# A bidirectional Mamba layer with its FFN: the last skip term moved into the state sum, one tail norm moved to VectorE, the head's first turn and projection in halves

## The chip, the cores and the metric

One NeuronCore of a Trainium2 chip. The metric is the device time of one execution in microseconds, the median of three runs. Engines are named as in the profile: PE is TensorE, PEld its weight loads, DVE VectorE, ACT ScalarE, POOL GpSimd, SP SyncE. TensorE's granted clock has two levels, 1.2 and 2.4 GHz; the profile gives it as a share of 2.4.

## The reference, cut to what matters

```python
def mamba(x, ...):                       # once forwards, once on the reversed sequence
    u, z = split(x @ in_w.T)             # 256 channels each
    u = silu(causal_conv4(u) + conv_b)
    dt, B, C = split(u @ xproj_w.T)      # rank 8, 16 states, 16 states
    dt = softplus(dt @ dt_w.T + dt_b)
    h[t] = exp(dt[t] * A) * h[t-1] + dt[t] * B[t] * u[t]     # 16 states per channel
    y[t] = sum_n(h[t, n] * C[t, n]) + D * u[t]               # D * u is the skip term
    return (y * silu(z)) @ out_w.T

xn = norm(layernorm(x)) * gamma + beta                        # x: 4 sequences x 512 tokens x 128
x = x + layernorm(layernorm(x) + mamba_f(xn) + reverse(mamba_b(reverse(xn))))
x = x + layernorm(ffn(layernorm(x)))     # ffn: (silu(x Wg) * (x Wu)) Wd, hidden 384, int weights / 127
```

All arithmetic is fp32, but for B's rows, which TensorE broadcasts as three bf16 parts.

## The kernel before, in words

**Tiling.** The work falls into 8 units, one for each sequence q and direction d (unit k = 2q + d), and each unit into 16 steps, one for each state n: 128 steps. In a step the channels lie on the partitions (two halves of 128) and the 512 positions in the free dimension, so that one VectorE scan of 128x1024 computes h for one state (L1313). Its inputs are the decay exp(dt A) from ScalarE (`exp`, L937, a ring of six) and dt B u, made in one of three ways: TensorE broadcasts row B into PSUM (`bcast`, L678, or L682 for the first four steps) and VectorE multiplies it by dt u (`mul_b`, L1294); or ScalarE scales the transposed dt u (`g`, L1048) and TensorE turns it back (`g_turn`, L705); or GpSimd multiplies (L1172). GpSimd multiplies h by C (`mul_c`, L1151), and TensorE adds the product to the sum over states by a transpose into the PSUM tile `ysum` (`fold`, L735), three steps behind the scan.

**Order.** `plan()` (L122) writes one list of stages; every engine walks through the same list and issues the stages that are its own, so the order in the list is the order in each engine's queue. `start` is the head, ahead of scan 0. `put(slot, ...)` weaves a stage in behind the scan of that step. `plan_banks()` (L306) gives each short-lived PSUM result one of the two `scr` banks, or, once the scans are over, one of six.

**Head.** The first sequence is loaded; VectorE takes the statistics, GpSimd the power -1/2, VectorE the four norms of 128 tokens each (L1377). TensorE transposes the four blocks (`turn`, L789), ScalarE scales them by gamma and beta into `xn_fwd` (L982). One half of the convolution is a plain projection (`u_raw`, L797), for which VectorE then makes the four tap passes (`conv_passes`, L1386 and L1393), the other half is four matmuls with folded taps (L809). Three warm-up matmuls (L664) stand between turn and projection, 14 ahead of the turn. ScalarE makes u (L991), TensorE the x projection (L830), ScalarE copies it to `xdbl` (L1005). Then `bc`: four small transposes of B and C (L840) and ScalarE's copy to `bc_t` (L1013); `dt_mm` (L849) and `dt` (L1021) for each half; `dtu` on VectorE (L1415). SyncE stores `xdbl` and reads C's rows back as broadcast tiles as soon as `xdbl` is read. Beside this VectorE takes the statistics of the other three sequences (`ln_var_rest`, L1369 and L1371), and GpSimd takes their powers (`ln_pow_next` L1183, `ln_pow_rest` L1187) and folds the taps of the backward direction (`fold_taps`, L1215). Behind scan 0 come `dtu_turn` (L713, L1036) and the turn of the first backward half, again L789.

**Tail.** The last two steps are scanned in two parts of 256 positions (L1332), part 1 of the tokens (blocks 2 and 3) first; `ysum` of the last unit has one bank for each part. The last c products of step 127 are VectorE's (L1343). Ahead of the last folds stands `skip` (L748), which writes D u for both parts into the gate's bank; `back` (L758) turns the copied sum and adds it there. Then for each part: gate (L1424), output projection (`oproj_base` L653, `oproj_mm` L880), layer norm 2 (`ln_stats` L1441, L1445, L1451, power on GpSimd L1262, the norm on VectorE as `ln_dve` L1465 or on ScalarE as `ln_shift` L1457 and `ln_act` L1083), the sum `add_attn` (L1473), layer norm 3, `turn_x1` (L890, and its copy on VectorE L1480), the FFN (L901, L1133, L1486, L911), layer norm 4, the last sum (L1492) and the store. Norm 2 is on VectorE for part 1 and on ScalarE for part 0. 16 warm-up matmuls (L664) stand ahead of the first `turn_x1`.

## Time and profile before

| | |
|---|---|
| runs | 456.19, 453.91, 454.21 us; median 454.21 |
| profiled execution | 457.79 us, its span 456.0 us |
| busy share of the span | PE 88%, DVE 92%, ACT 83%, POOL 87% |
| mean granted clock | 0.946 |
| first scan, last whole scan ends | 22.78 us, 422.7 us |

The span goes from the first instruction to the last; the execution's own time holds 1.79 us more around it. In the timeline and the chain of waits a row's first number is its start in us from the span's start, the second its time; "x4" groups neighbouring instructions of one line, and the time then reaches from the first one's start to the last one's end. An fp32 matmul shows as two records, a transpose as one. In brackets stands the idle time of the engine ahead of the row and what ended it. L12 is line 12 of the kernel.

### The profile page before, as it was taken

How to read it: one execution, taken by the hardware profiler on the slowest of the kernel's cores; microseconds unless marked ns; L12 is line 12 of the kernel's file. 1: busy time of each engine (PE TensorE's matmuls, PEld its weight loads, DVE VectorE, ACT ScalarE, POOL GpSimd, SP SyncE). 2: the span in 40 equal slices, each digit the busy share in tenths (PEclk: the TensorE clock that was granted, in tenths of full speed). 3: DMA queues.
4: the chain of work that ended last, by engine and by line, in shares of the span. 5: the costliest groups of instructions: out<-in, count | busy, mean ns of one | idle time of the engine just before them, and what ended most of it. 6: DMA issues, size and time to landing. Idle time of an engine off the chain costs nothing. (4 is left out here: it accounts for less than half of the span.)

```text
span 456.0 us, 6724 instructions
## 1 busy us (share of the span) xinstructions
PE 399.5 (88%) x2269; PEld 269.3 (59%) x2269; DVE 420.4 (92%) x343; ACT 378.0 (83%) x739; POOL 396.5 (87%) x239
## 2 busy tenths in 40 slices
PE   7769967997799799989999799979999797989985
PEld 3345544565666585644756585644756485557854
DVE  4999998899999999998999999988999999998774
ACT  3799998597968999987989999897989999978231
POOL 1689999978999899999979999999979999997622
PEclk9969997998799999988999999988999997999999
DMA  8542222313141222322232332322222323220001
GB/s 239 222 156 74 72 87 89 123 49 123 46 152 57 108 73 111 107 86 86 92 117 69 111 95 112 107 83 84 94 115 71 102 77 125 96 92 1 2 0 46
DMA packets 17633, 42.76 MB, mean 94 GB/s; under 512 B 1600, under 2 KB 7104, under 8 KB 17600
## 3 DMA queue, kind: packets, MB, share of 16 engines
q1 hardware_dynamic: 17600, 42.34, 26.6%
q8 instruction: 18, 0.29, 0.3%
q14 instruction: 15, 0.12, 0.1%
HBM read 40.76 MB, written 1.57 MB: 93 GB/s over the span
## 5 line engine op out<-in xcount | busy, mean ns | idle before, releaser
L1151 POOL TENSOR_TENSOR hq<-hq,c_tiles 128x1024 f32<-128x1024 f32 x126 | 295.7, 2370 | 21.2 <-DVE hq L1313 21.1
L1313 DVE TENSOR_TENSOR_SCAN hq<-da,bb 128x1024 f32<-128x1024 f32 x114 | 257.8, 2279 | 8.8 <-PE bb L705 1.7
L937 ACT ACTIVATE da<-dt,neg_a 128x511 f32<-128x511 f32 x232 | 150.4, 710 | 4.9 <-DVE hq L1313 4.7
L735 PE MATMUL ysum<-wts,hq 128*128 128x128 f32 x1016 | 139.9, 283 | 7.4 <-POOL hq L1151 7.3
L735 PEld LDWEIGHTS ysum<-wts,hq 128*128 128x128 f32 x1016 | 116.2, 144 | 32.7 <-issue 20.4
L1294 DVE TENSOR_TENSOR bb<-bb,dtu 128x1024 f32<-128x1024 f32 x78 | 94.4, 1210 | 5.8 <-PE bb L678 5.2
L1048 ACT ACTIVATE g<-dtu_t,bc_t 128x256 f32<-128x256 f32 x152 | 64.4, 498 | 0.5 <-ACT dtu_t L1036 0.5
L705 PE MATMUL bb<-wts,g 128*128 128x128 f32 x304 | 41.5, 281 | 4.4 <-DVE hq L1313 2.7
L705 PEld LDWEIGHTS bb<-wts,g 128*128 128x128 f32 x304 | 35.1, 144 | 13.5 <-issue 9.1
L678 PE MATMUL bb<-b_rows,pick 48*128 48x512 bf16 x74 | 29.7, 402 | 9.5 <-DVE hq L1313 9.5
L678 PEld LDWEIGHTS bb<-b_rows,pick 48*128 48x128 bf16 x74 | 6.9, 94 | 47.1 <-DVE hq L1313 25.3
L809 PE MATMUL scr<-xn_rev,wconv 128*128 128x512 f32 x64 | 30.9, 605 | 0.0
L1313 DVE TENSOR_TENSOR_SCAN hq<-bb,dbu 128x1024 f32<-128x1024 f32 x12 | 27.3, 2275 | 1.5 <-issue 1.5
L1172 POOL TENSOR_TENSOR dbu<-dtu,b_tiles 128x1024 f32<-128x1024 f32 x12 | 28.5, 2378 | 0.0
L809 PE MATMUL scr<-xn_fwd,wconv 128*128 128x512 f32 x56 | 28.1, 629 | 0.0
L901 PE MATMUL scr<-x_t,wffn 128*128 128x512 f32 (+1 forms) x44 | 24.0, 649 | 2.9 <-DVE hid L1486 1.5
L1262 POOL TENSOR_TENSOR rstd<-rstd,minus_half 128x4 f32<-128x4 f32 (+1 forms) x15 | 13.4, 893 | 13.8 <-DVE rstd L1451 13.1
L937 ACT ACT_TABLE_LOAD x17 | 21.8, 1283 | 0.4
L830 PE MATMUL scr<-u,wts 128*73 128x512 f32 x32 | 18.2, 700 | 2.6 <-ACT x_t L1128 2.0
L977 ACT ACTIVATE y_t<-ysum 128x512 f32<-128x512 f32 x16 | 8.7, 591 | 11.7 <-PE ysum L735 11.7
L1249 POOL TENSOR_TENSOR dtu<-dt,u 128x1024 f32<-128x1024 f32 x7 | 16.5, 2362 | 0.1
L819 PE MATMUL scr<-xn_fwd,wts 128*128 128x512 f32 x32 | 16.4, 637 | 0.0
(159 smaller groups left out, 491.8 us busy)
## 6 DMA issues: line engine op xcount, KB each, us to landing
c_tiles<-bc_rows_dram SPq DMA_DIRECT2D x64, 512.0 KB, 3.6
b_tiles<-bc_rows_dram SPq DMA_DIRECT2D x12, 256.0 KB, 4.3
x_res<-x_dram SPq DMA_DIRECT2D x1, 768.0 KB, 8.0
out_dram<-o SPq DMA_DIRECT2D x3, 256.0 KB, 2.3
wts<-packed_dram SPq DMA_DIRECT2D x1, 584.0 KB, 9.0
hid<-w_ffn_dram SPq DMA_DIRECT2D x1, 576.0 KB, 7.7
wconv<-conv_taps_dram SPq DMA_DIRECT2D x2, 256.0 KB, 4.2
wconv<-conv_taps_dram SPq DMA_DIRECT2D x1, 512.0 KB, 7.5
```

Of the source, the lines that this page charges most:

```text
L678: mm = nc.tensor.matmul(bb[:, i % BB_RING, 1, :], pick[0:PARTS * NS, n:n + 1].broadcast_to([PARTS * NS, P]), b_rows[:, k % 2, :], start=Tr ...
L705: mm = nc.tensor.matmul(bb[:, i % BB_RING, h, block(b)], g[:, n % G_RING, b, h, :], ident, start=True, stop=True, is_transpose=True)
L735: mm = nc.tensor.matmul(ysum[:, bank, at], products(i, a[1:])[:, h, block(b)], ident, start=opens, stop=(i % NS == NS - 1), is_transpose=T ...
L809: mm = nc.tensor.matmul(scratch(use), wconv[:, d, t, h * P:(h + 1) * P], src, start=(t == 0), stop=(t == TAPS - 1))
L830: mm = nc.tensor.matmul(scratch(use)[0:XROWS, :], wx[:, k % 2, h, :], u[:, k % U_RING, h, :], start=(h == first), stop=(h != first))
L901: signal_full(nc.tensor.matmul(scratch(use)[:, 0:at.stop - at.start], w[:, block(c)], x1_t[:, at], start=True, stop=True), use)
L937: ins = nc.scalar.activation(da[:, i % DA_RING, h, 1:SEQ], dt[:, k % 2, h, 1:SEQ], ACT.Exp, scale=neg_a[:, c:c + 1])
L1048: ins = nc.scalar.activation(g[:, m % G_RING, b], dtu_t[:, k % 2, b], ACT.Copy, scale=bc_t[:, k % 2, b, ROW_B + n:ROW_B + n + 1])
L1151: nc.gpsimd.tensor_tensor(hq[:, i % H_RING], hq[:, i % H_RING], c_tiles[:, n % C_RING, i % 2, :].unsqueeze(1).broadcast_to([P, 2, SEQ]), A ...
L1172: nc.gpsimd.tensor_tensor(dbu[:], dtu[:, k % 2], b_tiles[:, n % POOLED_RING].unsqueeze(1).broadcast_to([P, 2, SEQ]), ALU.mult).then_inc(s_ ...
L1294: nc.vector.tensor_tensor(bb[:, i % BB_RING], bb[:, i % BB_RING, 1, :].unsqueeze(1).broadcast_to([P, 2, SEQ]), dtu[:, k % 2], ALU.mult).th ...
L1313: nc.vector.tensor_tensor_scan(out=hq[:, i % H_RING].rearrange("p h t -> p (h t)"), data0=decay.rearrange("p h t -> p (h t)"), data1=dbu_t ...
```

## The change

The last unit's skip term is no longer a group of matmuls ahead of the last folds: eight matmuls of a block of u with the diagonal of D add it to `ysum` in the slot of step 116, behind fold 113, and `back` opens its bank itself. Norm 2 of part 0 goes from ScalarE (with the shift that it needs) to VectorE, behind `ln_dve` of norm 3 and ahead of the copy of `turn_x1`. In the head the four norms signal in pairs, the first turn goes in two halves to two banks, its activation and `u_raw` in two halves each. `bc` of unit 0 comes behind both `dt_mm` on TensorE, and its copy is VectorE's, between the two `dtu` products. On GpSimd `ln_pow_rest` comes ahead of the backward taps' product. No DMA is added, taken away or put elsewhere in SyncE's queue. Left out below are the declarations of semaphores and what follows from them.

```diff
@@ plan() @@
-              ("ln_var_rest",), ("fold_taps", 1), ("ln_pow_rest",)]
-    start += [("xproj_mm", 0, 1), ("xproj_mm", 0, 0), ("xproj", 0), ("bc", 0), ("dt_mm", 0, 0), ("dt_mm", 0, 1), ("dt", 0, 0), ("dt", 0, 1),
-              ("dtu", 0, 0), ("dtu", 0, 1)]
+              ("ln_var_rest",), ("ln_pow_rest",), ("fold_taps", 1)]
+    start += [("xproj_mm", 0, 1), ("xproj_mm", 0, 0), ("xproj", 0), ("dt_mm", 0, 0), ("dt_mm", 0, 1), ("dt", 0, 0), ("dt", 0, 1),
+              ("dtu", 0, 0), ("bc", 0), ("dtu", 0, 1)]
...
+    put(STEPS - NS + 4, ("skip", UNITS - 1))
     put(STEPS - 5, ("oproj_part_mm",), ("oproj_part",))
...
-            if i == STEPS - 1:
-                order += [("skip", UNITS - 1, r) for r in TAIL_PARTS]
...
-    order += [("ln_dve", 2, a), ("add_attn", q, a), *rstd(3, a), *rstd(2, b), ("ln_dve", 3, a), ("ln_shift", 2, q, b),
-              ("turn_x1", q, a), ("ln_act", 2, q, b), ("oproj", q, a), ("oproj", q, b), ("add_attn", q, b), *rstd(3, b)]
+    order += [("ln_dve", 2, a), ("add_attn", q, a), *rstd(3, a), *rstd(2, b), ("ln_dve", 3, a), ("ln_dve", 2, b),
+              ("turn_x1", q, a), ("oproj", q, a), ("oproj", q, b), ("add_attn", q, b), *rstd(3, b)]
@@ TensorE @@
                 elif stage == "skip":
-                    k, r = a
-                    use, n = ("gate", k, r), HALVES[r][1] - HALVES[r][0]
+                    k, = a
                     pe.wait_ge(s_diag, 1)
                     for h in range(2):
                         was_read(pe, ("conv_out", k, h))
-                    may_write(pe, use)
                     for h in range(2):
-                        nc.tensor.matmul(scratch(use)[:, h * n * P:(h + 1) * n * P], skip_diag[:, 1, h, :],
-                                         u[:, k % U_RING, h, ::-1][:, cols_of(LAST, r)], start=(h == 0), stop=False,
-                                         skip_group_check=True)
+                        for b in range(BLK):
+                            bank, at = by_part(h, b)
+                            nc.tensor.matmul(ysum[:, bank, at], u[:, k % U_RING, h, block(b)], skip_diag[:, 1, h, :],
+                                             start=False, stop=False, skip_group_check=True)
                 elif stage == "back" and a[0] == UNITS - 1:
                     k, r = a
                     use, (lo, hi) = ("gate", k, r), HALVES[r]
+                    may_write(pe, use)
                     pe.wait_ge(s_yout, 2 * k + turn_of(r) + 1)
...
-                                                  start=False, stop=(h == 1 and n == hi - lo - 1), is_transpose=True,
+                                                  start=(h == 0 and n == 0), stop=(h == 1 and n == hi - lo - 1), is_transpose=True,
...
+                elif stage == "turn" and a == (0, 0):
+                    pe.wait_ge(s_first, 16)
+                    may_write(pe, item)
+                    for r, bank in enumerate((scratch(item), ysum[:, 1, :])):
+                        pe.wait_ge(s_normed_first, r + 1)
+                        for b in range(*HALVES[r]):
+                            mm = nc.tensor.matmul(bank[:, block(b)], normed[:, 0, b, :], ident,
+                                                  start=True, stop=True, is_transpose=True)
+                        if r == 0:
+                            mm.then_inc(s_turn_first, 1)
+                    signal_full(mm, item)
...
-                    was_read(pe, ("turn", 0, 0))
-                    nc.tensor.matmul(bb[:, 1, 1, :], w_u_stage[:, 0, P:DI], xn_fwd[:, 0, PAD:PAD + SEQ],
-                                     start=True, stop=True).then_inc(s_u_raw, 1)
+                    for r, (lo, hi) in enumerate(HALVES):
+                        if r == 0:
+                            pe.wait_ge(s_xn_first, 1)
+                        else:
+                            was_read(pe, ("turn", 0, 0))
+                        mm = nc.tensor.matmul(bb[:, 1, 1, lo * P:hi * P], w_u_stage[:, 0, P:DI],
+                                              xn_fwd[:, 0, PAD + lo * P:PAD + hi * P], start=True, stop=True)
+                    mm.then_inc(s_u_raw, 1)
@@ ScalarE @@
+                elif stage == "turn" and a == (0, 0):
+                    for r, bank in enumerate((scratch(item), ysum[:, 1, :])):
+                        at = slice(HALVES[r][0] * P, HALVES[r][1] * P)
+                        if r == 0:
+                            act.wait_ge(s_turn_first, 1)
+                        else:
+                            written(act, item)
+                        ins = nc.scalar.activation(xn_fwd[:, 0, PAD:][:, at], bank[:, at], ACT.Identity,
+                                                   scale=col("gamma"), bias=col("beta"))
+                        if r == 0:
+                            ins.then_inc(s_xn_first, 1)
+                    signal_read(ins, item)
...
-                elif stage == "bc":
+                elif stage == "bc" and a[0] >= 1:
@@ VectorE @@
                     for b in range(BLK):
                         ins = nc.vector.tensor_scalar(normed[:, q, b, :], x_res[:, q, b, :], mean_in[:, q, b, 0:1],
                                                       rstd_in[:, q, 0, b:b + 1], ALU.subtract, ALU.mult)
-                    ins.then_inc(s_normed_first, 1)
+                        if b % 2:
+                            ins.then_inc(s_normed_first, 1)
...
+                elif stage == "bc" and a[0] == 0:
+                    written(dve, item)
+                    signal_read(nc.vector.tensor_copy(bc_t[:, 0].rearrange("p b n -> p (b n)"),
+                                                      scratch(item)[:, 0:BLK * 2 * NS]), item)
```

## Rows read from the trace of the kernel before

**Rows 1.** Windows: us, busy us of each engine, granted clock, DMA share, GB/s.

```profile
56.00:64.00 8.00, 4.82 (x36) 3.69 (x37) 7.82 (x6) 7.97 (x17) 7.77 (x9) 1.00 0.18 68
300.00:320.00 20.00, 18.57 (x84) 10.00 (x85) 16.48 (x12) 16.05 (x28) 19.25 (x13) 0.83 0.27 90
```

**Rows 2.** Timeline, head: start, us, engine, line, operation, idle before and releaser.

```profile
7.40 0.63 PE L789 MATMUL scr<-wts,normed 128*128 128x128 f32 x4 [1.82 <-DVE normed L1377]
...
8.06 0.78 ACT L982 ACTIVATE xn_fwd<-scr,wts 128x512 f32<-128x512 f32 x1 [4.00 <-PE scr L789]
...
8.99 1.10 PE L797 MATMUL bb<-xn_fwd,w_u_stage 128*128 128x512 f32 x2 [0.20 <-ACT xn_fwd L982]
```

**Rows 3.** Timeline from 16 us; the last row is of the waits.

```profile
16.05 0.68 ACT L1005 ACTIVATE xdbl<-scr,wts 73x512 f32<-73x512 f32 x1
...
16.79 0.30 PE L840 MATMUL scr<-wts,xdbl 32*128 32x32 f32 x2 [0.78 <-ACT xdbl L1005]
...
18.80 0.60 ACT L1021 ACTIVATE dt<-scr 128x512 f32<-128x512 f32 x1 [0.18 <-PE scr L849]
...
20.79 5.00 ACT L937 ACTIVATE da<-dt,neg_a 128x511 f32<-128x511 f32 x8
...
ACT dt L1021 <- PE scr L849: 0.7, 2, 0.5
```

**Rows 4.** Timeline, GpSimd and VectorE, 17.6 to 25 us.

```profile
17.68 2.34 POOL L1215 TENSOR_TENSOR wconv<-wconv,w_u_stage 128x1024 f32<-128x1024 f32 x1
17.75 2.30 DVE L1369 TENSOR_SCALAR rstd_in<-mean_in 128x8 f32<-128x8 f32 x1
...
19.97 0.16 DVE L1371 TENSOR_SCALAR rstd_in<-mean_in 128x8 f32<-128x8 f32 x1
20.04 1.30 DVE L1415 TENSOR_TENSOR dtu<-dt,u 128x512 f32<-128x512 f32 x2
...
20.20 3.27 POOL L1187 TENSOR_TENSOR rstd_in<-rstd_in,minus_half 128x16 f32<-128x16 f32 x1 [0.18 <-DVE rstd_in L1371]
...
22.78 2.29 DVE L1313 TENSOR_TENSOR_SCAN hq<-da,bb 128x1024 f32<-128x1024 f32 x1
```

**Rows 5.** Timeline, first dtu_t activation to the product of step 2.

```profile
25.70 1.05 ACT L1036 ACTIVATE dtu_t<-scr 128x512 f32<-128x512 f32 x2
...
26.42 1.09 PE L789 MATMUL scr<-wts,normed 128*128 128x128 f32 x4 [3.05 <-ACT dtu_t L1036]
...
27.30 1.06 PE L682 MATMUL bb<-wts,bc_t 128*128 128x128 f32 x4
...
28.50 1.21 DVE L1294 TENSOR_TENSOR bb<-bb,dtu 128x1024 f32<-128x1024 f32 x1
```

**Rows 6.** Timeline around step 118; a TensorE group of 16 records.

```profile
393.60 0.39 PE L678 MATMUL bb<-b_rows,pick 48*128 48x512 bf16 x1 [0.64 <-DVE hq L1313]
...
395.64 1.21 DVE L1294 TENSOR_TENSOR bb<-bb,dtu 128x1024 f32<-128x1024 f32 x1
...
421.20 1.95 PE L911 MATMUL scr<-wffn,hid 128*128 128x128 f32 x16
```

**Rows 7.** Tail: first row from the chain of waits, others the timeline.

```profile
425.79 1.88 PE scr L748 x8
...
429.66 0.69 DVE L1343 TENSOR_TENSOR hq<-hq,c_tiles 128x512 f32<-128x512 f32 x1
...
431.48 1.03 PE L735 MATMUL ysum<-wts,hq 128*128 128x128 f32 x8
...
431.68 0.69 DVE L1424 TENSOR_TENSOR gated<-scr,zs 128x512 f32<-128x512 f32 x1 [1.32 <-PE scr L758]
```

**Rows 8.** Timeline, tail: warm-up matmuls, norm of part 0, copy.

```profile
436.71 3.64 PE L664 MATMUL ysum<-minus_half 128*64 128x512 bf16 x16
...
439.82 0.81 ACT L1083 ACTIVATE ln_tile<-bb,shift,rstd 128x128 f32<-128x128 f32 x2 [5.16 <-DVE shift L1457]
...
440.76 0.42 DVE L1480 COPY x_t<-bb 128x256 f32<-128x256 f32 x1 [0.98 <-PE bb L890]
```

More of the change, by code:

```diff
@@ L295, in plan @@
     return order
-PRODUCERS = {"tap": ("conv_out", 3), "xproj_mm": ("xproj", 2), "dt_mm": ("dt", 3), "conv_passes": ("conv_out", 3), "back": ("gate", 3), "skip": ("gate", 3),
+PRODUCERS = {"tap": ("conv_out", 3), "xproj_mm": ("xproj", 2), "dt_mm": ("dt", 3), "conv_passes": ("conv_out", 3), "back": ("gate", 3),
              "oproj_base": ("oproj", 3), "oproj_mm": ("oproj", 3), "oproj_part_mm": ("oproj_part", 1),
@@ L457, in mamba_sandwich @@
         s_normed_first = sem("first_normed_done")
+        s_turn_first = sem("first_half_turned")
+        s_xn_first = sem("first_half_scaled")
         s_u_raw = sem("first_u_half_projected")
@@ L468, in mamba_sandwich @@
         s_shift = sem("ln3_shift_done")
-        s_tail_shift = [sem(f"ln{w}_tail_shift_done") for w in range(2, 5)]
+        s_tail_shift = sem("ln3_tail_shift_done")
         s_neg_mean = sem("negated_input_mean_done")
@@ L550, in normed_ready @@
             if q == 0:
-                eng.wait_ge(s_normed_first, 1)
+                eng.wait_ge(s_normed_first, 2)
             else:
@@ L1076, in _ @@
                     else:
-                        act.wait_ge(s_tail_shift[w - 2], 1)
+                        act.wait_ge(s_tail_shift, 1)
                     for b in range(*parts_of(q)[r]):
@@ L1458, in _ @@
                                                    scalar=-1.0, in1=rstd[:, w - 2, q, at], op0=ALU.mult,
-                                                   op1=ALU.mult).then_inc(s_tail_shift[w - 2], 1)
+                                                   op1=ALU.mult).then_inc(s_tail_shift, 1)
                 elif stage == "ln_dve":
```

## The prediction

> **What bounds the kernel now.** I read the page's shares first, then windows over the span, then the timeline by engine for the first 30 us and the last 45, and last the chain of waits. VectorE runs the state scans nearly without a gap from 22.8 us to 424, so the middle is VectorE's, except where TensorE's granted clock is low. In [rows 1] the stretch from 300 to 320 us has a mean granted clock of 0.83, and VectorE is busy 16.48 us of 20; at the rate from 56 to 64 us (7.82 of 8, clock 1.00) it would be 19.55, so 3.1 us were lost. The change touches nothing there. What it can shorten is the part before the scans settle and the part after the last one. In the head, one activation, one TensorE pass and one VectorE pass follow each other with nothing beside them [rows 2, 3]. In the tail TensorE is the engine that all wait for [rows 7]: VectorE sits 1.32 us idle in front of the gate of part 1.
>
> **The head, step by step.** *Norm, turn and projection in halves.* Now the four transposes (0.63 us) wait for all four norms, the activation takes 0.78, and the projection starts 0.20 us after its warm-up matmuls have ended, at 8.99 [rows 2]. With halves the first two transposes lie under the third and fourth norm, so the turn ends about 0.25 us sooner (two of its four), the three warm-up matmuls with it, and the projection finds its first half scaled; the second half (about 0.5 us of activation for 256 columns) ends near 8.3, ahead of the warm-ups' end at about 8.54. So the projection starts at 8.54 in place of 8.99: 0.45 us. It ends at 9.64 and not at 10.09, and the first convolution pass with it. At least 0.2 (the wait alone), at most 0.6. The passes, both activations of u, the table load and xdbl follow without slack, xdbl from 16.05 to 15.6.
>
> *dt ahead of B and C.* Before each dt activation ScalarE waited for TensorE, 0.5 and 0.2 us [rows 3]. TensorE spends about 0.2 us on the four small transposes there (0.30 for two records that overlap dt's). Without them dt comes 0.2 us sooner. The copy that ScalarE gives up lay in the wait. Sum on ScalarE: 0.65 us, table load and exps from 20.14 and not 20.79. The copy of B and C now sits on VectorE between the two dtu products; I take 0.25 us for 128 columns, between the 0.16 of a tiny operation [rows 4] and the 0.42 of a 256-column copy [rows 8]. It hides: dtu 1 waits for dt 1, which ends at 18.77.
>
> *GpSimd's order.* Now the tap product (2.34 us) runs on GpSimd from 17.68, and a VectorE operation on 8 elements that starts beside it takes 2.30 us, to 20.05; both dtu products stand behind it [rows 4]. With the powers first, this operation costs 0.16, like its neighbour at 19.97. VectorE then does dtu 0 at 18.0, the copy, dtu 1 at 18.95, and the first b product at 19.7. Scan 0 waits for exp 0 (20.14 + 1.25 = 21.4) and starts at 21.45 in place of 22.78: 1.33 us sooner. On GpSimd: powers 17.7 to 21.0, taps to 23.3, still ahead of its first c product at 23.75. SyncE's queue gains 0.45 by the earlier xdbl and is late for nothing.
>
> *What is late next.* Not all of 1.33 arrives. The b product of step 2 started at 28.50, and its broadcast ended at 28.36, with 0.1 us to spare [rows 5]. This broadcast stands on TensorE behind the turn of the backward half, which waited 3.05 us for the first dtu_t activation; that one stands behind four exps and so moves by 0.65. The b product thus comes at 27.78. **Head: 0.7 us**, with a new VectorE idle of 0.5 us in front of that product. From there VectorE ran without a gap, and GpSimd and TensorE follow it.
>
> *The rule of the ports.* In [rows 4] GpSimd's powers started at 20.20, and the second dtu product ran from 20.69 beside them in its usual 0.65 us: no block. The Trainium skill says otherwise ("SBUF — State Buffer", section "Who interferes with whom"): a VectorE instruction with two SBUF inputs and a GpSimd instruction that reads SBUF exclude each other, and whichever issues second fully blocks. The 2.30 us agrees with it, the dtu product under the powers doesn't. I go by the row; the other way is rival A.
>
> **Slot 4.** The skip term was 1.88 us of the chain at the end and now is 8 matmuls of 128 columns in the slot of step 116. The same form and count (16 records) takes 1.95 at 421.20, some 1.85 before the next can start [rows 6]. TensorE waited 0.64 us for VectorE in front of the broadcast of step 118, at 393.60; so it moves by 1.2 to 394.8, ends at 395.2, and its product was due at 395.64: 0.4 us to spare. What is queued behind (fold 114, the two turns back) gives the rest back in TensorE's later waits for scans. Cost 0; at a low clock, where everything doubles, up to 1.9.
>
> **The tail.** TensorE loses 1.88 us, so the folds of part 1, their copy and the turn back come 1.87 sooner. The gate of part 1 cannot: VectorE's last c product ends at 430.35 [rows 7], and the gate moves from 431.68 to 430.4. The fold of step 127, part 0, needs the same product: from 430.39 it takes 0.6, ending at 430.99, where now the folds end at 432.51. That is 1.52, and projection, statistics, powers and part 0 all follow it. At least 1.3 (the idle), at most 1.88.
>
> *The norm on VectorE.* Now ScalarE's two blocks take 0.81 us and end at 440.63; the sum that reads them stands on VectorE behind a copy that waits for TensorE until 440.76, because the 16 warm-up matmuls (3.64 us from 436.71) stand in front of its turn [rows 8]. On VectorE the norm needs no more than ScalarE's 0.81, in the 0.98 us in which VectorE idles, and the shift falls away. So 0, and up to 0.4 lost if it comes late. **Tail: 1.5 us.**
>
> **Sum.** 0.7 + 0 + 1.5 = 2.2 us. The profiled execution took 457.79 (span 456.0 and 1.79 around it); it should be 455.6. It is 3.58 above the median of 454.21, which is more time in low clock or the profiler, not a part that is changed. From the median: **452.0 us**. A measurement can tell about 0.5% from nothing, 2.27 us: my sum lies on that edge.
>
> **Rivals.**
> A. *The ports lock under the powers.* dtu 0, due at 18.0, waits until 21.0; scan 0 starts at 23.9, 1.1 late, and the head loses 1.1. 1.5 - 1.1 = 0.4 gained: 453.8. Against it, the dtu row. 0.1.
> B. *The broadcast of step 2 isn't late*, since turn and broadcast run at full clock: 0.63 for four transposes, as at 7.40, and not 1.09, as at 26.42. The head gives 1.3, in all 2.8: 451.4. TensorE idles as long ahead of it as now, so 0.08.
> C. *Slower: the tail at low clock.* The skip matmuls were the last ones that are not transposes before the projection. Now some 5.2 us of pure transposes and waits stand there. If the clock falls before 431, base, projection, turn back, second projection and warm-ups (7 us of TensorE on the chain) run their first 4.5 us at half rate: +4.5 - 2.2, 456.5. It decides from 2.2 us of doubled work on. Against: from 56 to 64 us TensorE was busy 4.82 of 8, nearly all transposes, at 1.00 [rows 1]. 0.06.
> D. *A low stretch more* in the middle, since all is shifted by 0.7 us: +3.1 - 2.2 = 455.1. The runs before span 453.91 to 456.19. 0.12. *One less*: 448.9, 0.07.
> E. *The halves bring nothing*, the projection still waits for a late second half: 452.5. 0.07.
> The forecast: 0.5.
>
> **Chances.** The forecast, with a noise of about 0.8 us (the runs before: 453.91, 454.21, 456.19), falls half on each side of 451.94: 0.25 and 0.25. Faster: 0.25 + B 0.07 + one less 0.07 + of E and D 0.03 = 0.42; slower (over 456.48): half of C and of D's upper end, 0.07; the same: 0.51. The range leaves out the lesser case and C: 450.2 to 454.9, the forecast's own 451.0 to 453.2.
>
> **What would show it.** Right: projection at 8.5; exps at 20.1; the 8-element operation at 0.16; scan 0 at 21.4, an idle of 0.5 before the b product of step 2; no VectorE wait near 394; the first part's gate at VectorE's c product without idle; last fold to last sum as long as before. Wrong: a dtu product of over 1 us (A); a granted clock under 1 after 428 (C); VectorE busy under 17 of 20 us in a stretch where it wasn't (D).

## The result and the profile after

Over 19 runs of each kernel the changed one takes **452.84 us** (450.52 to 454.52) and the one before 454.89 (453.08 to 457.72). The ratio is 0.9957, with a 95% interval of 0.994 to 0.9973: 0.43% or 1.96 us less. The interval leaves out 1, so the gain is real, and it lies inside the half per cent that the prediction took as the least that can be told from nothing. The forecast was 2.2 us less. The profiled execution took 452.48 us (span 450.7, mean granted clock 0.945).

First the head of the changed kernel, from the timeline: start, us, engine, line, operation, and the idle time before it with its releaser. These rows answer to [rows 2 to 5].

```profile
6.26 1.11 DVE L1407 TENSOR_SCALAR normed<-x_res,mean_in,rstd_in 128x128 f32<-128x128 f32 x4 [1.21 <-POOL rstd_in L1207]
7.01 0.41 PE L788 MATMUL scr<-wts,normed 128*128 128x128 f32 x2 [0.90 <-DVE normed L1407]
...
7.46 0.57 ACT L1003 ACTIVATE xn_fwd<-scr,wts 128x256 f32<-128x256 f32 x1 [3.51 <-PE scr L788]
...
8.56 1.14 PE L814 MATMUL bb<-xn_fwd,w_u_stage 128*128 128x256 f32 x4
8.78 0.19 DVE L1441 TENSOR_SCALAR neg_a<-neg_a 128x64 f32<-128x64 f32 x1 [0.80 <-ACT neg_a L971]
9.74 0.75 DVE L1417 TENSOR_SCALAR y_t<-bb,wts 128x509 f32<-128x509 f32 x1 [0.76 <-PE bb L814]
...
17.37 0.17 DVE L1399 TENSOR_SCALAR rstd_in<-mean_in 128x8 f32<-128x8 f32 x1
17.55 1.08 ACT L1051 ACTIVATE dt<-scr 128x512 f32<-128x512 f32 x2 [1.21 <-PE scr L867]
17.69 2.90 POOL L1217 TENSOR_TENSOR rstd_in<-rstd_in,minus_half 128x16 f32<-128x16 f32 x1 [0.36 <-DVE rstd_in L1401]
18.18 0.69 DVE L1450 TENSOR_TENSOR dtu<-dt,u 128x512 f32<-128x512 f32 x1 [0.57 <-ACT dt L1051]
19.13 1.97 PE L683 MATMUL bb<-wts,bc_t 128*128 128x128 f32 x8 [0.44 <-DVE bc_t L1444]
20.03 5.00 ACT L955 ACTIVATE da<-dt,neg_a 128x511 f32<-128x511 f32 x8
20.29 1.23 DVE L1324 TENSOR_TENSOR bb<-bb,dtu 128x1024 f32<-128x1024 f32 x1 [0.61 <-PE bb L683]
22.02 2.29 DVE L1343 TENSOR_TENSOR_SCAN hq<-da,bb 128x1024 f32<-128x1024 f32 x1 [0.51 <-DVE bb L1324]
...
27.74 1.21 DVE L1324 TENSOR_TENSOR bb<-bb,dtu 128x1024 f32<-128x1024 f32 x1
```

The projection starts at 8.56 (forecast 8.54), the exps at 20.03 (20.14), the 8-element operation takes 0.17 us, and the dtu product runs beside GpSimd's powers in 0.69: no block. The product of step 2 comes at 27.74 and not at 28.50, 0.76 sooner (forecast 0.72). On the way two things differ: the broadcasts in front of product 0 took 1.97 us where they took 1.09 before, with a granted clock of 0.50 from 19.1 to 21 us (1.00 under the same broadcasts before), and scan 0 started 0.50 us behind the end of product 0, at 22.02 and not at 21.45.

The slot of step 116, timeline; it answers to [rows 6]. The first row is work that TensorE did at the low clock just before, where a group of this form takes 1.88 us at the full one; the second is the fold behind it:

```profile
382.73 3.78 PE L837 MATMUL scr<-xn_fwd,wts 128*128 128x512 f32 x4
...
386.30 1.53 PE L736 MATMUL ysum<-wts,hq 128*128 128x128 f32 x8
...
389.41 1.95 PE L749 MATMUL ysum<-skip_diag,u 128*128 128x128 f32 x16
391.29 0.39 PE L679 MATMUL bb<-b_rows,pick 48*128 48x512 bf16 x1
391.72 1.23 DVE L1324 TENSOR_TENSOR bb<-bb,dtu 128x1024 f32<-128x1024 f32 x1 [0.40 <-PE bb L679]
```

VectorE now idles 0.40 us in front of product 118, which had no wait before. The tail, timeline; it answers to [rows 7, 8]:

```profile
420.00 2.42 DVE L1362 TENSOR_TENSOR_SCAN hq<-da,bb 128x256 f32<-128x256 f32 x4
...
425.77 0.73 DVE L1373 TENSOR_TENSOR hq<-hq,c_tiles 128x512 f32<-128x512 f32 x1
425.86 1.35 PE L736 MATMUL ysum<-wts,hq 128*128 128x128 f32 x8
426.43 0.68 DVE L1459 TENSOR_TENSOR gated<-scr,zs 128x512 f32<-128x512 f32 x1
...
428.59 0.49 DVE L1476 BATCH_NORM_STATS2 stats<-bb 128x6 f32<-128x128 f32 x2 [1.49 <-PE bb L898]
...
434.33 0.73 DVE L1500 TENSOR_SCALAR ln_tile<-bb,mean_var,rstd 128x128 f32<-128x128 f32 x2 [0.33 <-POOL rstd L1292]
...
435.46 0.42 DVE L1515 COPY x_t<-bb 128x256 f32<-128x256 f32 x1 [0.41 <-PE bb L908]
...
447.96 0.42 DVE L1527 TENSOR_TENSOR o<-x_res,ln_tile 128x256 f32<-128x256 f32 x1
```

The gate (426.43) has lost its 1.32 us of idle time. From the first part scan to the first statistics it is now 428.59 - 420.00 = 8.59 us; before it was 433.89 - 423.89 = 10.00. That is 1.41 us, where 1.52 was forecast. From the end of the last fold to the start of the last sum it takes 20.75 us in both kernels, as forecast. The chain of waits (start, us, engine, tile, line, records) shows what is left there; the 1.88 us of skip matmuls at the head of [rows 7] are gone from it:

```profile
421.91 2.63 PE ysum L736 x24
...
431.49 3.57 PE ysum L665 x16
435.46 0.42 DVE x_t L1515
```

**The middle is another matter.** From the product of step 2 to the first part scan it is 392.26 us after (420.00 - 27.74) and 395.39 before (423.89 - 28.50): 3.1 us less, which no part of the account can give. The windows (us, busy us of each engine, granted clock, DMA share, GB/s) of after at the two stretches of [rows 1]:

```profile
56.00:64.00 8.00, 6.23 (x36) 5.23 (x36) 7.82 (x5) 7.96 (x17) 7.78 (x9) 0.79 0.17 68
300.00:320.00 20.00, 18.66 (x102) 11.22 (x101) 18.39 (x13) 17.98 (x31) 19.46 (x13) 0.95 0.29 96
```

In the first stretch the clock was 0.79 and not 1.00, and VectorE was busy 7.82 us all the same. So the prediction's reading, that the middle is VectorE's except where the granted clock is low, holds for its second stretch and not for this one, where TensorE was busy only 6.23 of 8 us. In the second stretch VectorE is busy 1.9 us more at a clock of 0.95 than before at 0.83. Experiment 11 shows that this is not fixed by the code: with all of the change's code in the middle it had the slow pattern again.

### The profile page after: what moved, and what is told of

Same layout as the page of the kernel before. It is cut to its first block and busy times, and to the rows that moved or that the text cites. A ratio compares the mean times of both kernels' runs of the same rounds, so it can differ in the third digit from the quotient of the medians.

```text
span 450.7 us, 6742 instructions
## 1 busy us (share of the span) xinstructions
PE 400.9 (89%) x2279; PEld 274.3 (61%) x2279; DVE 419.0 (93%) x345; ACT 376.1 (83%) x737; POOL 395.8 (88%) x239
## 5 line engine op out<-in xcount | busy, mean ns | idle before, releaser
L1181 POOL TENSOR_TENSOR hq<-hq,c_tiles 128x1024 f32<-128x1024 f32 x126 | 295.5, 2369 | 18.0 <-DVE hq L1343 17.6
L736 PE MATMUL ysum<-wts,hq 128*128 128x128 f32 x1016 | 143.0, 286 | 4.3 <-POOL hq L1181 4.2
L736 PEld LDWEIGHTS ysum<-wts,hq 128*128 128x128 f32 x1016 | 118.5, 146 | 30.3 <-issue 20.1
L706 PE MATMUL bb<-wts,g 128*128 128x128 f32 x304 | 42.5, 285 | 4.9 <-DVE hq L1343 2.7
L679 PEld LDWEIGHTS bb<-b_rows,pick 48*128 48x128 bf16 x74 | 6.9, 93 | 44.1 <-issue 22.4
L827 PE MATMUL scr<-xn_rev,wconv 128*128 128x512 f32 x64 | 32.8, 638 | 0.0
L919 PE MATMUL scr<-x_t,wffn 128*128 128x512 f32 (+1 forms) x42 | 20.3, 580 | 3.7 <-DVE hid L1521 1.8
L848 PE MATMUL scr<-u,wts 128*73 128x512 f32 x32 | 16.4, 637 | 2.6 <-ACT x_t L1158 2.0
L827 PEld LDWEIGHTS scr<-xn_rev,wconv 128*128 128x128 f32 x64 | 12.0, 208 | 9.5 <-issue 9.5
L1028 ACT ACTIVATE zs<-scr 128x512 f32<-128x512 f32 x16 | 9.6, 598 | 9.3 <-PE scr L837 9.3
```

The source lines that it names most:

```text
L679: mm = nc.tensor.matmul(bb[:, i % BB_RING, 1, :], pick[0:PARTS * NS, n:n + 1].broadcast_to([PARTS * NS, P]), b_rows[:, k % 2, :], start=Tr ...
L706: mm = nc.tensor.matmul(bb[:, i % BB_RING, h, block(b)], g[:, n % G_RING, b, h, :], ident, start=True, stop=True, is_transpose=True)
L736: mm = nc.tensor.matmul(ysum[:, bank, at], products(i, a[1:])[:, h, block(b)], ident, start=opens, stop=(i % NS == NS - 1), is_transpose=T ...
L827: mm = nc.tensor.matmul(scratch(use), wconv[:, d, t, h * P:(h + 1) * P], src, start=(t == 0), stop=(t == TAPS - 1))
L848: mm = nc.tensor.matmul(scratch(use)[0:XROWS, :], wx[:, k % 2, h, :], u[:, k % U_RING, h, :], start=(h == first), stop=(h != first))
L919: signal_full(nc.tensor.matmul(scratch(use)[:, 0:at.stop - at.start], w[:, block(c)], x1_t[:, at], start=True, stop=True), use)
```

## The experiments

Each kernel is the changed one with the edit shown, except where the kernel before is named. Since the inputs land at slightly different times, times of the head are counted from the start of the norms on VectorE. Product 2 is VectorE's b product of step 2, the pass is the first convolution pass, and the last column is the distance from pass to first exp. This table is worked out from the timelines, one execution for each kernel.

| kernel | pass | first exp | scan 0 | product 2 | exp - pass |
|---|---|---|---|---|---|
| before | 3.98 | 14.65 | 16.64 | 22.36 | 10.67 |
| after | 3.48 | 13.77 | 15.76 | 21.48 | 10.29 |
| e2 halves back | 3.99 | 14.29 | 15.83 | 21.89 | 10.30 |
| e3 B, C first | 4.09 | 14.76 | 16.12 | 22.36 | 10.67 |
| e4 taps first | 3.47 | 13.77 | 17.24 | 22.96 | 10.30 |
| e5 turn later | 4.14 | 14.43 | 16.44 | 22.16 | 10.29 |
| e9 negation later | 3.48 | 13.78 | 15.32 | 21.38 | 10.30 |
| e10 only GpSimd | 3.98 | 14.65 | 16.02 | 22.26 | 10.67 |
| e11 12 warm-ups | 3.97 | 14.26 | 15.80 | 21.87 | 10.29 |
| e12 e9 and e11 | 3.47 | 13.77 | 15.30 | 21.38 | 10.30 |

**1. The skip term back at the end.**

```diff
-    put(STEPS - NS + 4, ("skip", UNITS - 1))
+            if i == STEPS - 1:
+                order += [("skip", UNITS - 1, r) for r in TAIL_PARTS]
```

> The changed kernel with only the skip term put back ahead of the last folds. My theory: the gain of the tail is the skip's 1.88 us capped by VectorE's last c product. From the first part scan of step 126 to the first statistics of norm 2 it takes 10.0 us again (8.6 with the change), VectorE idles about 1.3 us before the first gate, and the 0.4 us that the b product of step 118 waits for its broadcast is gone. The time: +1.0 us on the changed kernel. Rival: TensorE is not what the tail waits for, so the stretch stays at 8.6 and the time is unchanged; or the slot of step 116 costs as much as the tail gains, and the time is unchanged though the tail is longer.

Measured: 454.11 us (12 runs) beside 455.09, ratio 0.9977 (0.9948 to 1.0007), about 1 us less than before and 0.9 more than the changed kernel by the ratios, whose intervals overlap. Timeline of its tail:

```profile
419.47 2.42 DVE L1363 TENSOR_TENSOR_SCAN hq<-da,bb 128x256 f32<-128x256 f32 x4
...
427.26 0.69 DVE L1460 TENSOR_TENSOR gated<-scr,zs 128x512 f32<-128x512 f32 x1 [1.33 <-PE scr L760]
...
429.47 0.49 DVE L1477 BATCH_NORM_STATS2 stats<-bb 128x6 f32<-128x128 f32 x2 [1.52 <-PE bb L899]
```

It is 10.00 us from the part scan to the statistics again, the gate waits 1.33 us again, and the wait in front of product 118 is gone. So the move is worth 1.41 us at the end, and its slot cost 0.40 in the changed kernel's trace.

**2. Norm, turn and projection in one piece again** (the three special cases of the halves taken out).

> The changed kernel with the first turn, its activation and the first projection whole again. My theory: the projection starts about 0.45 us later after the norms (2.85 us after the first norm's start and not 2.30), and everything up to the b product of step 2 moves by the same 0.45 to 0.55. Rival: another wait (the taps, the negation of A, or statistics of the other sequences) takes it up, and exp 0 still comes at about 20.0 us.

Measured: the projection starts 2.85 us after the norms (after: 2.30), the first exp 14.29 (13.77), so the halves are worth 0.52 to 0.55 there. At product 2 only 0.41 of it is left. The negation of exp(A) was early in both traces, so nothing else moved the pass. One execution: 454.51 us.

**3. B and C ahead of dt, copied by ScalarE.**

```diff
-start += [..., ("dt_mm", 0, 0), ("dt_mm", 0, 1), ("dt", 0, 0), ("dt", 0, 1), ("dtu", 0, 0), ("bc", 0), ("dtu", 0, 1)]
+start += [..., ("bc", 0), ("dt_mm", 0, 0), ("dt_mm", 0, 1), ("dt", 0, 0), ("dt", 0, 1), ("dtu", 0, 0), ("dtu", 0, 1)]
```

> The changed kernel with B and C ahead of dt on TensorE again and their copy on ScalarE. My theory: dt comes 0.2 us later after xdbl, so exp 0, the dtu_t activation, the broadcast of step 2 and its product come 0.2 us later; scan 0 comes not later but sooner by up to 0.3, since the broadcast of step 0 is no longer the last thing it waits for. Rival: the order of B, C and dt is worth more than 0.2 us, or nothing, because the exps are bound by something else.

Measured: the first exp at 14.76 and not at 13.77. Only part of that is the order; this run's convolution pass itself was late by 0.61. The last column of the table parts the two: the stretch from pass to exp is 10.67 us in the three kernels with B and C first and 10.29 or 10.30 in all the others, experiments 1, 6, 7 and 8 too. **The order is worth 0.38 us at the first exp**, and not the 0.2 that was expected. At product 2 it is 0.27 (18.27 us behind the pass here, 18.00 in the changed kernel; 17.90 in experiment 9, where the broadcasts ran at the full clock), as the first scan comes 0.25 later behind the pass with the new order (12.28 and 12.03). ScalarE's rows, timeline:

```profile
18.15 0.60 ACT L1051 ACTIVATE dt<-scr 128x512 f32<-128x512 f32 x1 [0.49 <-PE scr L867]
...
18.94 0.60 ACT L1051 ACTIVATE dt<-scr 128x512 f32<-128x512 f32 x1 [0.18 <-PE scr L867]
```

With dt first the two activations run as one group of 1.08 us, where they take 1.39 here. One execution: 452.8 us.

**4. GpSimd's tap products ahead of its powers.**

```diff
-              ("ln_var_rest",), ("ln_pow_rest",), ("fold_taps", 1)]
+              ("ln_var_rest",), ("fold_taps", 1), ("ln_pow_rest",)]
```

> The changed kernel with the backward taps' product ahead of the powers on GpSimd again. My theory: the 8-element operation of VectorE takes over 2 us again, both dtu products come 1.9 us later, scan 0 starts at about 23.2 and not 22.0, scan 1 follows, and the b product of step 2 comes at 28.7 to 29.0 in place of 27.74: VectorE is then the one that is late, by about 1 us, and the broadcast of step 2 waits ready. Rival: the b product of step 2 stays at 27.7, since only the broadcast sets it, and the new order of GpSimd is worth nothing; or the operation is short again, since it was no port but something else that held it.

Measured, timeline:

```profile
17.36 2.34 POOL L1245 TENSOR_TENSOR wconv<-wconv,w_u_stage 128x1024 f32<-128x1024 f32 x1
17.44 2.30 DVE L1399 TENSOR_SCALAR rstd_in<-mean_in 128x8 f32<-128x8 f32 x1
```

The 2.30 us are back, product 2 comes 1.48 us later than in the changed kernel (22.96 and 21.48), later than the 0.96 to 1.26 that were expected and even 0.6 later than in the kernel before: the copy of B and C now stands on VectorE too, behind the held operation, and all broadcasts wait for it. One execution: 456.09 us.

**5. The turn of the backward half behind the broadcast of step 2.**

```diff
-put(at, ("dtu_turn", 0, 0), ("dtu_turn", 0, 1), ("pick",), ("split", 0), ("turn", 0, 1))
-put(at + 1, ("b_rows", 0))
+put(at, ("dtu_turn", 0, 0), ("dtu_turn", 0, 1), ("pick",), ("split", 0))
+put(at + 1, ("turn", 0, 1), ("b_rows", 0))
```

> The changed kernel with the first backward turn on TensorE and ScalarE put behind the broadcast of step 2 (slot 1, ahead of b_rows). My theory: what caps the head is that turn, which waits for the first dtu_t activation with the broadcast of step 2 queued behind it. Then the broadcast ends by about 25.5 us, VectorE's idle of 0.5 us before the b product of step 2 is gone, that product starts at 27.2 and all scans after it are 0.5 us sooner; scan 3 starts at 32.05 and not 32.57. Rival: the broadcast of step 3 or the first backward taps, now later, take its place, and scan 3 is where it was.

Measured: 456.19 us (12 runs) beside 454.33, ratio 1.0023 (0.999 to 1.0056), some 3 us above the changed kernel, and the two intervals don't meet. The expectation (0.5 us less) failed. Timeline:

```profile
24.89 0.65 PE L683 MATMUL bb<-wts,bc_t 128*128 128x128 f32 x4 [1.89 <-DVE hq L1343]
...
28.27 1.21 DVE L1324 TENSOR_TENSOR bb<-bb,dtu 128x1024 f32<-128x1024 f32 x1
...
31.77 3.75 PE L827 MATMUL scr<-xn_rev,wconv 128*128 128x512 f32 x4 [1.51 <-ACT xn_rev L1012]
...
36.89 2.29 DVE L1343 TENSOR_TENSOR_SCAN hq<-da,bb 128x1024 f32<-128x1024 f32 x1 [1.51 <-PE bb L706]
```

The broadcast is ready 2.7 us ahead of its product, which gains nothing: the product comes 5.72 us after scan 0, as in the changed kernel, since scan 0 itself was late. And the turn had better cover where it was: its activation now stands behind more exps (30.75 and not 26.78), the taps of the backward half follow late, and scan 4 waits 1.51 us. From scan 3 to scan 5 it takes 7.97 us here (41.06 - 33.09) and 5.68 in the changed kernel (38.25 - 32.57), 2.3 us more. How much of that is the order isn't shown: TensorE's granted clock was 0.50 from 26 to 36 us (0.68 in the changed kernel), and the four taps took 3.75 us where such a group takes 1.88 at the full clock, which adds more than scan 4's wait.

**6. The operations swapped so that the dtu products run beside a tap product.**

```diff
-("ln_var_rest",), ("ln_pow_rest",), ("fold_taps", 1)]
+("fold_taps", 1)]
-("dtu", 0, 0), ("bc", 0), ("dtu", 0, 1)]
+("dtu", 0, 0), ("bc", 0), ("dtu", 0, 1), ("ln_var_rest",), ("ln_pow_rest",)]
```

> The changed kernel with the tap product first on GpSimd and VectorE's two variance operations and GpSimd's last powers behind the dtu products. So a tap product (two SBUF inputs) runs on GpSimd from 17.4 to 19.8, while VectorE's first dtu product (two SBUF inputs) is due at 18.2. By the rule of the lock the dtu product shows about 1.6 us more than its 0.69 (or starts so much later), and ends near 20.4. Rival: only VectorE's two-port form (one tensor input, the 8-element operation) is held up by GpSimd, and the dtu product takes 0.69 us as it does under the powers.

Measured, timeline:

```profile
17.58 2.34 POOL L1245 TENSOR_TENSOR wconv<-wconv,w_u_stage 128x1024 f32<-128x1024 f32 x1
...
18.47 2.00 DVE L1450 TENSOR_TENSOR dtu<-dt,u 128x512 f32<-128x512 f32 x1 [0.85 <-ACT dt L1051]
```

The same dtu product takes 2.00 us beside GpSimd's product and ends 0.55 after it, where it takes 0.69 beside the powers. One execution: 455.16 us.

**7. The last unit's skip term left out** (the output lacks D u of the last backward unit): the `put(..., ("skip", UNITS - 1))` removed and nothing in its place.

> The changed kernel without the last unit's skip term: the eight matmuls of step 116 are left out and nothing stands for them, so the output lacks D u of the last backward unit. My theory: the slot costs 0.4 us where TensorE comes late out of a low stretch of its clock and 0 else; in this run the b product of step 118 doesn't wait, and the time is 0 to 0.4 us below the changed kernel, within noise. Rival: 1.95 us of TensorE's work in that slot cost more than the wait that it makes (folds and turns back behind it), and the time falls by 1 us or more; or the tail too is shorter, which it should not be.

Measured: 452.24 us (12 runs) beside 454.33, ratio 0.9949 (0.993 to 0.9969). No wait at product 118; part scan to statistics 8.58 us, as after. The intervals of this kernel and of the changed one overlap, so the times can't price the slot; the traces do, with a wait of 0 to 0.64 us at product 118 (below). The rival, 1 us or more, shows neither in this median (0.4 us under the changed kernel's by the ratios) nor in the waits.

**8. The norm of part 0 back on ScalarE.**

```diff
-... *rstd(2, b), ("ln_dve", 3, a), ("ln_dve", 2, b), ("turn_x1", q, a), ("oproj", q, a), ...
+... *rstd(2, b), ("ln_dve", 3, a), ("ln_shift", 2, q, b), ("turn_x1", q, a), ("ln_act", 2, q, b), ("oproj", q, a), ...
```

> The changed kernel with norm 2 of part 0 on ScalarE again. My theory: worth nothing, since the sum that reads it stands behind a copy that waits for the turn behind 16 warm-up matmuls: from the end of the warm-ups to the last sum (12.9 us) nothing changes, and the copy still waits for TensorE. Rival: VectorE's norm ahead of the copy is worth something, and the stretch from the first statistics of norm 2 to the end is longer by the 0.3 us that the copy waits less.

Measured: 452.71 us in one execution. Timeline:

```profile
435.68 0.42 DVE L1515 COPY x_t<-bb 128x256 f32<-128x256 f32 x1 [0.98 <-PE bb L908]
```

The copy comes 15.46 us after the first part scan in both kernels; here VectorE idled 0.98 us ahead of it and there 0.41. The last sum starts 27.96 us after the part scan in both. The move is worth nothing.

**9. The negation of exp(A) behind the first convolution pass.** The table had shown that the pass started late, by up to 0.7 us, in most runs with halves. On VectorE a 0.2 us operation on exp(A) stands ahead of the pass, and exp(A) waits for the transfer of the early weights.

```diff
-... *taps(0, 0), ("neg_a",), ("conv_passes", 0, 1),
+... *taps(0, 0), ("conv_passes", 0, 1), ("neg_a",),
```

> The changed kernel, with VectorE's negation of exp(A) put behind the first convolution pass. In the changed kernel this 0.2 us operation stands ahead of the pass and waits for the transfer of the early weights, so that the pass came 0.1 to 0.6 us behind the projection's end in six of the runs with halves. Theory (this transfer caps what the halves bring): the pass starts at most 0.1 us behind the end of the projection, whatever the transfer does; first exp 13.7 to 13.9 us after the start of the norms on VectorE; against the changed kernel in the same call 0 to 0.8 us less, 0.4 in the mean. Rival 1 (the transfer also holds something else, the second pass or the exps): pass early, first exp unchanged. Rival 2 (the order is worth nothing since conv_out waits for table or copy anyway): the same as rival 1 with an idle on ScalarE in front of conv_out.

Measured: 452.38 us (11 runs) beside 454.62, ratio 0.9961 (0.994 to 0.9981). Timeline:

```profile
9.47 0.75 DVE L1417 TENSOR_SCALAR y_t<-bb,wts 128x509 f32<-128x509 f32 x1 [1.76 <-PE bb L814]
9.71 0.26 ACT L971 ACTIVATE neg_a<-wts 128x64 f32<-128x64 f32 x1 [1.50 <-DMA wts<-packed_dram]
...
21.31 2.29 DVE L1343 TENSOR_TENSOR_SCAN hq<-da,bb 128x1024 f32<-128x1024 f32 x1 [0.52 <-ACT da L955]
...
27.37 1.23 DVE L1324 TENSOR_TENSOR bb<-bb,dtu 128x1024 f32<-128x1024 f32 x1 [0.26 <-PE bb L683]
```

The weights were late here (9.71) and the pass was not; the first exp is at 13.78, as forecast. In the time it shows no gain over the changed kernel's ratio, which it couldn't: 0.1 to 0.5 us is less than these intervals can tell apart.

**10. The kernel before with GpSimd's order alone** (the edit of experiment 4 the other way round).

> The kernel before with one edit of the change alone: GpSimd's first powers ahead of its tap products. Theory (this edit removes the 2.30 us operation, but what stands behind the exps then sets the end): the 8-element operation takes 0.16 to 0.2 us; dtu product 0 at about 18.5 and not 20.04; scan 0 right behind exp 0, at 22.2 to 22.7 (22.78 before), because exp 0 still comes at about 20.8; product of step 2 at 28.3 to 28.5, so alone it gives 0 to 0.4 us, where taking it out of the changed kernel cost 1.5: the two parts of the head are worth more together than apart. Rival (the lock was the bound by itself): scan 0 at 21.4 and product 2 a full 1.3 us sooner.

Measured, timeline:

```profile
17.94 0.17 DVE L1369 TENSOR_SCALAR rstd_in<-mean_in 128x8 f32<-128x8 f32 x1
...
22.34 2.29 DVE L1313 TENSOR_TENSOR_SCAN hq<-da,bb 128x1024 f32<-128x1024 f32 x1 [0.69 <-ACT da L937]
...
28.58 1.23 DVE L1294 TENSOR_TENSOR bb<-bb,dtu 128x1024 f32<-128x1024 f32 x1 [0.44 <-PE bb L682]
```

The operation is down to 0.17, scan 0 comes 0.62 sooner, and product 2 only 0.10 (22.26 and 22.36), now with 0.44 us of idle time. The theory holds. The execution took 458.31 us, with a long middle (395.85 us from product 2 to the first part scan).

**11. Twelve warm-up matmuls in the tail, not sixteen** (`("warm", 16)` to `("warm", 12)`).

> The changed kernel with 12 warm-up matmuls in the tail and not 16 (0.9 us less of TensorE). Theory (these matmuls, and not the norm, bound the copy of part 0's turned block, which is why the norm's move gave nothing): the copy comes as soon as VectorE's norm 2 is through, some 0.4 us sooner than 15.46 us after the first part scan, and the end with it; granted clock stays 1.00. Rival (the warm-ups hold the clock up): a granted clock under 1 in the tail and matmuls of the feed-forward part at twice their time, +2 us or more.

Measured: 452.25 us (12 runs) beside 454.62, ratio 0.9958 (0.9933 to 0.9982). Timeline of the tail, and a window of its middle:

```profile
424.55 2.42 DVE L1362 TENSOR_TENSOR_SCAN hq<-da,bb 128x256 f32<-128x256 f32 x4
...
435.97 2.78 PE L665 MATMUL ysum<-minus_half 128*64 128x512 bf16 x12
...
439.53 0.41 DVE L1515 COPY x_t<-bb 128x256 f32<-128x256 f32 x1
```

```profile
300.00:324.00 24.00, 22.33 (x103) 12.40 (x104) 20.47 (x14) 20.05 (x36) 23.25 (x15) 0.86 0.29 91
420.00:450.00 30.00, 25.59 (x177) 21.29 (x177) 24.10 (x64) 9.21 (x26) 13.56 (x12) 1.00 0.03 10
```

The copy comes 14.98 us after the part scan and no longer waits for TensorE: 0.48 sooner, and so does the last sum (27.47 and 27.96), at a granted clock of 1.00. The first window tells more still. VectorE is busy 20.47 of 24 us at a clock of 0.86, and the kernel before showed, in the same stretch,

```profile
300.00:324.00 24.00, 21.83 (x102) 12.06 (x102) 20.48 (x15) 20.05 (x35) 23.25 (x15) 0.86 0.28 96
```

where the changed kernel showed 22.39 at 0.96. This execution's middle took 396.57 us (424.55 - 27.98), longer than before's 395.39, with the changed kernel's code in it.

**12. Both edits, 9 and 11.**

> The changed kernel with both of these edits: the negation behind the first convolution pass, and 12 warm-up matmuls. If both theories hold the gains add, as they lie in head and tail: 0.4 to 0.8 us below the changed kernel, which is under the bound that tells from no change against it but 2.5 us below the kernel before, ratio about 0.994. If either rival holds, the same as the changed kernel or slower.

Measured: **451.61 us** (6 runs, 451.43 to 452.14) beside 454.62, ratio 0.9936 (0.9913 to 0.9959). First exp at 13.77, product 2 at 21.38, the copy 14.93 us after the part scan (434.56 - 419.63). It has the lowest median of the study, and its interval lies wholly under 1; against the changed kernel (0.9957, up to 0.9973) the intervals overlap, so that the 0.5 to 1 us between them rests on the traces.

## Why the prediction held, point by point

**The sum.** 0.7 + 0 + 1.5 = 2.2 us were forecast. The traces give 0.88 for the head (22.36 - 21.48 in the table; 0.76 on the clock of the execution, since its norms began 0.12 later), -0.4 for the slot and 1.4 for the tail: 1.9. The runs say 1.96, with an interval of 1.2 to 2.7. Two of these terms are not the same in every execution. In the five traces with the changed head as it is (after, 1, 7, 8, 11) product 2 comes at 21.48 to 21.87, in the mean 0.63 sooner than before; and of the ten traces with the skip term in its slot four show a wait, 0.18 in the mean. By these means the sum is 0.63 - 0.18 + 1.41 = 1.9 again. For experiment 12 the same account gives 0.98 for the head and 1.94 for the tail (the copy at 14.93 and not at 16.87), 2.9, with the slot's wait gone in its trace, and the runs say 2.9. That the predicted 452.0 lies 0.8 under the median comes mostly from its base: the kernel before has 454.89 as the median of 19 runs and 454.21 as that of the three that were known.

**Halves, 0.45 by the forecast.** They are worth 0.50 at the pass (3.98 to 3.48) and 0.52 at the exp (experiment 2). The size is right, but a bound was missing: the convolution pass waits for the later of the projection and the negation of exp(A), that is, of a transfer. Before, the negation had ended at 9.67 and the projection at 10.09; with the projection half a microsecond sooner, the transfer set the start of the pass in seven of the nine runs that have the halves and the negation in front (pass at 3.65 to 4.14). In the mean of those nine the pass stands at 3.80, beside 3.98 or 3.99 in the three traces without halves, so the halves brought 0.18 and not 0.50. The forecast's 0.45 is thus too high for most executions, and that dt gave more than forecast makes up for it: partly luck. Rival E got its effect there by a way that it didn't name. Experiment 9 takes this bound away and 11 against 12 prices it: 0.49 at the exp.

**dt ahead of B and C, 0.2 by the forecast.** The step is mis-sized; it is 0.38. I had counted the first dt's gain and taken the copy to lie in the wait. The first dt does come only 0.08 sooner, but the pair then takes 1.08 us and not 1.39, as the second lost its wait (0.18) and the two overlap.

**GpSimd's order.** As forecast: 0.17 for the operation, product 0 free of it. The dtu product beside the powers took 0.69, so rival A is out. Experiment 6 shows the two-input product held while GpSimd's product ran (2.00 us), and experiment 4 an operation with one tile input (2.30 us). With both the section of the Trainium skill that the prediction names ("SBUF — State Buffer", section "Who interferes with whom") agrees: it gives the shared ports to one engine for a whole instruction, and it lists `tensor_scalar`, which the 8-element operation is, among those that can take both of VectorE's ports. The prediction set the 2.30 us beside the section's rule on two inputs, and this operation has one. With the powers the section does not agree: they read SBUF as well, and the product beside them isn't held. Here the measurement decides. Why the powers don't hold it wasn't tried.

**What is late next.** The cap that this step named is real, but in the changed kernel's trace it was not the last one. Product 2 has two caps. One is the scan's: in every kernel without a wait it comes 5.71 to 5.73 us after scan 0. The other is the one that the forecast named, the turn and the broadcast behind the dtu_t activation, which stands behind four exps: wherever the product waited for TensorE (experiments 2, 3, 9, 10, 11, 12) it came 7.60 or 7.61 us after the first exp. In the changed kernel's trace the caps are 21.48 and 21.37, so the scan's came last, and the idle of 0.5 that was forecast isn't there; with scan 0 at 15.3 it is, as 0.26. So that the product came at 27.74, beside 27.78 in the forecast, is partly luck: scan 0 was 0.57 late, which just filled the idle. Experiment 5 removed the second cap in an execution where the first one was the later, and so could not win; it lost by what it moved. By both caps GpSimd's order alone can give no more than 22.36 - (14.65 + 7.60) = 0.11, and gave 0.10, while its removal from the whole costs 1.48, since there the copy of B and C stands behind the held operation. The edits of the head must not be priced one by one.

**Scan 0 at 21.45.** It came at 22.02, by two things. The broadcasts before product 0 ran at the low clock (1.97 us and not 1.09). In experiments 9 and 12 they took 1.09 behind the same idle of TensorE (0.43 and 0.44 us), and scan 0 came 0.4 us sooner by the table. What put the clock down in the one and not in the other isn't shown. And product 0 to scan 0 has a gap of 0.5 us, with exp 0 done by then (about 21.3, while product 0 ends at 21.52). What it is stays **open**: it is there in every kernel with the copy on VectorE whose scan isn't held longer by the exp, and it was 0.10 before. No run took it apart.

**Slot 4, cost 0.** Product 118 waited 0.40 us in the profiled execution, 0.29, 0.43 and 0.64 in those of experiments 3, 8 and 11, and not at all in the other six with the skip term there (2, 4, 5, 6, 9, 12). What parts them is the first fold behind the z projection: it took 1.41 to 1.91 us in the four that waited, so a part of it still ran at the low clock there, and 1.04 to 1.20 in the six. The forecast had 0.4 us to spare at the full clock and named up to 1.9 at a low one: the cases that happened lie between, as the low stretch ended just ahead of the slot and left TensorE late in some.

**The tail.** 1.41 for 1.52, capped by VectorE's c product as forecast: the gate follows it without idle. The norm is worth 0, hidden by the warm-ups, which experiments 8 and 11 show from both sides. Whether it would be worth something with 12 of them, where the copy no longer waits for TensorE, wasn't run. The clock was 1.00 from 428 to 440 us, so rival C is out. The 4.5 us at half rate that this rival reckoned with come from no row. The one low stretch of the kernel before that its windows show best, from 72 to 80 us with granted clocks of 0.52 and 0.62 in its halves, holds some 7 us of low clock (an estimate from these two), so the rival's price was open.

**Rival D.** One low stretch less (0.07) is what the profiled execution looks like: its middle is 3.1 us shorter. Nothing shows that to be the change's doing. The middle took between 390.5 us (experiment 7: 418.38 - 27.85) and 396.6 us (experiment 11) in executions of kernels that are nearly the same there, and the medians leave no room for it. Two profiled executions differ by 5.3 us (457.79 and 452.48) where the medians differ by 2; only 1.9 of it belongs to the edits.

## What to carry to other kernels

Where several engines wait for one another in a short head, find every cap on the instruction that counts (here: scan 0 plus 5.72, first exp plus 7.60) before pricing an edit; the gain is the movement of the latest one, and an edit that gave 0.10 alone cost 1.48 when it was taken out of the whole. Ask of each shortened step what else its follower waits for, transfers included, even behind an unrelated 0.2 us operation in the same queue. Count durations between two instructions inside one execution, and leave out the stretches in which only the granted clock differs.

## What the hardware showed that was not expected

- VectorE's product of two SBUF tiles is held beside GpSimd's tensor product and not beside its powers: the dtu product took 2.00 us and 0.69. The first scan of the changed kernel, with one of its inputs in PSUM, ran beside the same GpSimd product (20.55 to 22.92) and took its usual 2.29.
- GpSimd's last powers took 2.90 us in twelve traces, and 3.27 in the two where they start while the first dtu product runs (before [rows 4], experiment 4).
- An operation on 8 elements with a single tile input is held as well, 2.30 us for 0.17.
- Kernels with nearly the same code have a middle of 390.5 to 396.6 us from one execution to the next; the granted clock of the stretch from 300 to 324 us was 0.86 in four traces (before, 6, 10, 11), 0.96 in the changed kernel's and 1.00 in experiment 7's, and VectorE was busy 20.2 to 20.5 us of it, 22.4 and 23.0. Twelve executions of one kernel (experiment 11) took 450.78 to 456.57 us.
- Four warm-up matmuls fewer (16 to 12) left the clock at 1.00 from 428 to 440 us.
